# Moving the sampling of a convolution kernel from an expert stage to the stage after it, on one core

## The chip, the cores and the metric

One core of one Trainium2 chip runs the whole program. The metric is the device time of one execution in microseconds; the kernel before took 3562.75 us (median of three runs, 3560.17 to 3565.22). TensorE does the matrix products, ACT (ScalarE), DVE (VectorE) and POOL (GpSimd) work elementwise, and SP issues most of the transfers.

## The reference, cut to what matters

The reference is a decoder of two layers on 4 x 512 tokens of width 256. In each layer an attention, a cross attention and a mixture of experts follow each other, each with a residual and a layer norm behind it. Two of the pieces matter here. The first is layer 0's mixture, in which each token goes to 2 of 8 experts:

```python
g = jax.nn.softmax(h @ Wr, axis=-1)
top2_w, top2_idx = jax.lax.top_k(g, 2)
top2_w = top2_w / jnp.sum(top2_w, axis=-1, keepdims=True)
hid = jax.nn.relu(jnp.einsum('bsh,ehf->bsef', h, W1))
expert_out = jnp.einsum('bsef,efh->bseh', hid, W2)
```

The second is the long convolution of layer 1. Its kernel K depends on weights alone, so it can be made long before it is needed:

```python
dtA = dt[:, None] * A
dC = C * (jnp.exp(dtA) - 1.0) / A
powers = jnp.exp(dtA[:, :, None] * jnp.arange(L))
K = 2.0 * jnp.einsum('dn,dnl->dl', dC, powers).real
Kf = jnp.fft.rfft(K, n=n, axis=-1)
```

d is one of 256 channels, n one of 64 states, l one of 512 positions. A value K[d, l] is called a tap here.

## The kernel before, in words

`l0_ffn` runs layer 0's mixture in four stages: routing, sorting the tokens by expert, the experts (`l0_experts`), and combining with the norm (`l0_combine_and_norm`). Each stage is a block: all engines start it together, and each runs its own list of instructions in order, with waits on semaphores between them.

**The taps.** For every channel the position is split as l = low + 32 x high. For each state (real and imaginary parts on 128 partitions) V holds the powers of the 32 low parts and U those of the 16 high parts, with the coefficients. The taps of one channel are then one product of a 128x32 and a 128x16 matrix. DVE and ACT make V and U in the expert stage, 32 channels at a time: eight chunks (CHUNKS = 8, CW = 32 channels), each in four pieces (`piece`, `growth`, `waves` of `ConvolutionKernel`). One float32 product is two matmul instructions in the trace, so a chunk is 64 of them. V is a tile of its own; U lies in G.branch, which nobody else uses until the stage after the combine.

**The expert stage** (`l0_experts`) runs over 39 slots of 128 sorted rows (SLOTS). For each slot j TensorE does the hidden layer of slot j+1 (L1453, 32 instructions), the transposes of the rows of slot j+2 (L1442) and the output of slot j (L1464, 16 instructions). ACT applies the relu (L1501) and copies rows and results (L1494, L1507); DVE brings the expert's first weights (L1532) and makes a piece of V or U; SP loads rows and the second weights (1 MB a slot) and stores the results. In the second of every four slots from slot 5 on, TensorE also does `taps(c)` for the chunk finished before (L1473), into the PSUM tile pk. Two slots later DVE copies it out with four strided copies (L1543), each a quarter of the high parts into 32 partitions of K.taps. So there are eight slots with taps and 31 without.

**The combine stage** (`l0_combine_and_norm`). POOL issues 32 gathers (L2846), two experts' results for each of 16 token tiles. For each of four batches DVE waits for the batch's eight gathers, adds the weighted results (L2916), takes mean and variance, waits for ACT's square root (`root(b)`, L2888, with one table load), and scales x (L2929). TensorE then transposes the batch (`turn(b)`, L2867) and ACT copies the transposes out (`copies(b)`, L2894). Besides, the taps are taken to the spectrum: eight transforms (L2856), each of eight 128x256 matmul instructions with the DFT matrix, which SP loads when the stage starts; ACT keeps each result (L2883), and SP stores all of it once the eighth is there (L2936). The order is written by hand. On TensorE: transforms 0 to 3, turn(0), transforms 4 to 7, turn(1), turn(2), turn(3). On ACT: keep 0 to 3, root(0), copies(0), keep 4 to 7, root(1), copies(1), and so on.

`made` in `l0_experts` counts the steps of the coefficients, from which the taps' wait for DVE is worked out.

Of the kernel before, what the change touches and what calls it, by code (L numbers as in the profile page):

```python
# [15 lines left out]
B, S, D = 4, 512, 256  # L16
# [25 lines left out]
def buffers(nc, ctx, tag):  # L42

    def sb(name, shape, dt=F32):
        return ctx.enter_context(nc.sbuf_tensor(f"{tag}_{name}", shape, dt))

    def ps(name, shape):
        return ctx.enter_context(nc.psum_tensor(f"{tag}_{name}", shape, F32))

    def sem(name):  # L50
        return ctx.enter_context(nc.semaphore(f"{tag}_{name}"))

    return sb, ps, sem
# [908 lines left out]
LO, HI = 32, 16  # L962
MAGIC = 1.5 * 2 ** 23
TWO_PI = 6.283185
CHUNKS = 8
CW = D // CHUNKS
# [409 lines left out]
def l0_experts(nc, G, R, K):  # L1376

    with ExitStack() as ctx:
        sb, ps, sem = buffers(nc, ctx, "f0")
# [10 lines left out]
        px = ps("px", [P, KD, P])  # L1390
        ph = [ps(f"ph{i}", [P, 512]) for i in range(2)]
        py = [ps(f"py{i}", [P, D]) for i in range(2)]
        pk = ps("pk", [LO, CW, HI])
        tapped, taps_read = sem("tapped"), sem("taps_read")
        made = K.steps[0]
        xs_loaded = [sem(f"xs_loaded{i}") for i in range(3)]
        w2_loaded = [sem(f"w2_loaded{i}") for i in range(2)]
        y_stored = [sem(f"y_stored{i}") for i in range(3)]
# [3 lines left out]
        with nc.Block() as block:  # L1402
# [32 lines left out]
            @block.tensor  # L1435
            def _(pe):
                def turn_rows(j):
                    pe.wait_ge(xs_loaded[j % 3], 16 * (j // 3 + 1))
                    if j >= 1:
                        pe.wait_ge(x_ready, j)  # L1440
                    for k in range(KD):
                        ins = pe.transpose(px[:, k, :], xs[:, j % 3, k * P:(k + 1) * P], G.ident[:])  # L1442
                    ins.then_inc(x_turned, 1)

                def hidden(j):
                    pe.wait_ge(x_ready, j + 1)
                    for half in range(2):
                        if j >= 1:
                            pe.wait_ge(h_done, 2 * (j - 1) + half + 1)
                        pe.wait_ge(w1_brought, 2 * j + half + 1)  # L1450
                        for f in range(HF):
                            for k in range(KD):
                                ins = pe.matmul(ph[half][:, f * P:(f + 1) * P], first[half][:, k, f * P:(f + 1) * P], xsT[:, j % 2, k, :],  # L1453
                                                start=(k == 0), stop=(k == KD - 1))
                        ins.then_inc(h_full, 1)

                def out(j):
                    pe.wait_ge(w2_loaded[j % 2], 16 * (j // 2 + 1))
                    if j >= 2:
                        pe.wait_ge(y_done, j - 1)  # L1460
                    for f in range(FT):
                        if f % HF == 0:
                            pe.wait_ge(h_done, 2 * j + f // HF + 1)
                        ins = pe.matmul(py[j % 2][:], hT[j % 2][:, f * P:(f + 1) * P], w2[:, j % 2, f, :],  # L1464
                                        start=(f == 0), stop=(f == FT - 1))
                    ins.then_inc(y_full, 1)

                def taps(c):
                    pe.wait_ge(K.dve_steps, made + K.STEPS * (c + 1))
                    if c >= 1:  # L1470
                        pe.wait_ge(taps_read, c)
                    for i in range(CW):
                        ins = pe.matmul(pk[:, i, :], K.V[:, CW * c + i, :], K.U[:, CW * c + i, :], start=True, stop=True)  # L1473
                    ins.then_inc(tapped, 1)

                turn_rows(0)
                turn_rows(1)
                hidden(0)
                for j in range(SLOTS):
                    if j + 1 < SLOTS:  # L1480
                        hidden(j + 1)
                    if j + 2 < SLOTS:
                        turn_rows(j + 2)
                    out(j)
                    if j % K.PIECES == 1 and 1 <= j // K.PIECES <= CHUNKS:
                        taps(j // K.PIECES - 1)

            @block.scalar
            def _(act):
# [34 lines left out]
            @block.vector  # L1524
            def _(dve):
                def bring(j):
                    e = dve.value_load(R.expert[0:1, j:j + 1], min_val=0, max_val=E0 - 1)
                    for half in range(2):
                        if j >= 1:
                            dve.wait_ge(h_full, 2 * (j - 1) + half + 1)  # L1530
                        w = R.w1[:, bass.ds(e, 1), :, half * 512:half * 512 + 512].rearrange("p a k f -> p (a k) f")
                        dve.tensor_copy(first[half], w).then_inc(w1_brought, 1)  # L1532

                dve.wait_ge(R.w1_loaded, 16 * E0)
                bring(0)
                for j in range(SLOTS):
                    if j + 1 < SLOTS:
                        bring(j + 1)
                    c = j // K.PIECES - 1
                    if j % K.PIECES == 3 and 0 <= c < CHUNKS:  # L1540
                        dve.wait_ge(tapped, c + 1)
                        for a in range(4):
                            ins = dve.tensor_copy(K.taps[32 * a:32 * a + 32, :, CW * c:CW * c + CW],  # L1543
                                                  pk[:, :, :].rearrange("l c (j a) -> l a j c", a=4)[:, a])
                        ins.then_inc(taps_read, 1)
                    if 0 <= (j - 1) // K.PIECES < CHUNKS:
                        K.piece(dve, (j - 1) // K.PIECES, (j - 1) % K.PIECES)

# [1274 lines left out]
def l0_combine_and_norm(nc, G, R, K):  # L2823

    with ExitStack() as ctx:
        sb, ps, sem = buffers(nc, ctx, "cn")
# [3 lines left out]
        rstd = sb("rstd", [P, TT])  # L2830
        pf = [ps(f"pf{i}", [P, 512]) for i in range(2)]
        pT = [ps(f"pT{i}", [P, NT, P]) for i in range(2)]
        dft_in, spectrum, kept, stored = sem("dft_in"), sem("spectrum"), sem("kept"), sem("stored")
        moments, rooted, x_ready = sem("moments"), sem("rooted"), sem("x_ready")
        turned, copied, dve_steps = sem("turned"), sem("copied"), sem("dve_steps")
# [5 lines left out]
        with nc.Block() as block:  # L2841
# [8 lines left out]
            @block.tensor  # L2850
            def _(pe):
                def transform(m):
                    if m >= 2:
                        pe.wait_ge(kept, m - 1)
                    for k in range(NT):
                        ins = pe.matmul(pf[m % 2][:, 0:D], dft[:, k, m * P:(m + 1) * P], K.taps[:, k, :],  # L2856
                                        start=(k == 0), stop=(k == NT - 1))
                    ins.then_inc(spectrum, 1)

                def turn(b):  # L2860
                    pe.wait_ge(x_ready, NT * (b + 1))
                    for k in range(KD):
                        n = b * KD + k
                        if n >= 2:
                            pe.wait_ge(copied, n - 1)
                        for q in range(NT):
                            ins = pe.transpose(pT[n % 2][:, q, :], G.x[:, b * NT + q, k * P:(k + 1) * P], G.ident[:])  # L2867
                        ins.then_inc(turned, 1)

                pe.wait_ge(dft_in, 16)  # L2870
                for m in range(FT):
                    transform(m)
                turn(0)
                for m in range(FT, 2 * FT):
                    transform(m)
                for b in range(1, B):
                    turn(b)

            @block.scalar
            def _(act):  # L2880
                def keep(m):
                    act.wait_ge(spectrum, m + 1)
                    act.copy(kf[:, m, :], pf[m % 2][:, 0:D]).then_inc(kept, 1)  # L2883

                def root(b):
                    r = slice(b * NT, (b + 1) * NT)
                    act.wait_ge(moments, b + 1)
                    act.activation(std[:, r], rstd[:, r], ACT.Sqrt).then_inc(rooted, 1)  # L2888

                def copies(b):  # L2890
                    for k in range(KD):
                        n = b * KD + k
                        act.wait_ge(turned, n + 1)
                        act.copy(G.xT[:, k, b * S:(b + 1) * S], pT[n % 2][:].rearrange("p a b -> p (a b)")  # L2894
                                 ).then_inc(copied, 1)

                for m in range(FT):
                    keep(m)
                root(0)
                copies(0)  # L2900
                for m in range(FT, 2 * FT):
                    keep(m)
                for b in range(1, B):
                    root(b)
                    copies(b)

# [592 lines left out]
```

## Time and profile before

| | |
|---|---|
| median of three runs | 3562.75 us |
| the profiled execution | 3564.6 us |
| its span, first to last instruction | 3562.8 us |
| mean granted TensorE clock | 0.823 of full |
| TensorE busy | 2771.1 us (78%) |
| DVE busy | 2386.4 us (67%) |
| ACT busy | 1118.4 us (31%) |
| POOL busy | 997.6 us (28%) |

The profile is of one execution. Its times are microseconds from the first instruction. A share of busy time is a mean over stages with different limits; here the two stages of the change lie at 671 to 976 (experts) and 979 to 1032 (combine). PEclk is the granted clock of TensorE as a share of full speed: 1.00 is 2.4 GHz, 0.50 is 1.2 GHz. In a timeline, neighbouring instructions of a kind are merged into one row; the ends of matmuls are modelled, so the spacing of starts is the better measure.

### The profile page before, as it was taken

Reading aid. Unit: us, or ns where it says so; the run is one execution under the profiler, and the core shown is the slowest. Engines: PE = TensorE matmul, PEld = TensorE weight load, DVE = VectorE, ACT = ScalarE, POOL = GpSimd, SP = SyncE. Lnnn points to the kernel's source line nnn. Section 1 sums busy time; section 2 is a strip of 40 time slices with the busy share of each in tenths; the row PEclk is TensorE's granted clock in tenths of the full one; section 3 lists DMA queues with packets and bytes.
Section 4 is the critical chain, followed back from the end, with each engine's and each line's share of the span. In section 5 each row is a group of like instructions: output and inputs, shape, how many; then the busy total and the mean of one; then the engine's idle time right before and its main releaser. Section 6 shows DMA issues by size and latency. Waiting matters only on the chain. (4 is left out here: it accounts for less than half of the span.)

```text
span 3562.8 us, 43681 instructions
## 1 busy us (share of the span) xinstructions
PE 2771.1 (78%) x12600; PEld 1905.2 (53%) x12600; DVE 2386.4 (67%) x8897; ACT 1118.4 (31%) x2893; POOL 997.6 (28%) x1242
## 2 busy tenths in 40 slices
PE   4665995499957667767787668765479999999999
PEld 2223564499834345535464445454436656666666
DVE  4996565466334999899989998999767635212112
ACT  1113562244313333433343334332232123222221
POOL 2552000300032454545454545455312210000000
PEclk7556996699976788787867886867679999999999
DMA  2000002455532211212122211111020032212212
GB/s 96 0 0 14 6 1 104 129 170 164 162 131 92 76 59 63 65 65 69 54 72 68 69 55 67 60 54 35 1 93 1 1 89 67 79 53 63 77 51 68
DMA packets 180780, 235.56 MB, mean 66 GB/s; under 512 B 35761, under 2 KB 138869, under 8 KB 180286
## 3 DMA queue, kind: packets, MB, share of 16 engines
q1 hardware_dynamic: 177470, 224.37, 19.7%
q0 software_dynamic: 3072, 8.39, 0.7%
q8 instruction: 103, 1.69, 0.2%
q14 instruction: 135, 1.11, 0.1%
HBM read 170.57 MB, written 62.13 MB: 65 GB/s over the span
## 5 line engine op out<-in xcount | busy, mean ns | idle before, releaser
L1883 PE MATMUL a_pat<-a_kp,a_probs 128*128 128x128 f32 x1344 | 292.8, 392 | 237.7 <-POOL a_kp L2102 232.7
L1883 PEld LDWEIGHTS a_pat<-a_kp,a_probs 128*128 128x128 f32 x1344 | 259.6, 288 | 317.3 <-POOL a_kp L2102 300.0
L2141 POOL TENSOR_SCALAR a_probs<-a_mixed,a_best 128x120 f32<-128x120 f32 (+12 forms) x208 | 302.4, 1454 | 251.8 <-DVE a_best L2208 115.8
L3408 DVE TENSOR_TENSOR tl_hT<-tl_act_out,tl_gate 128x512 f32<-128x512 f32 x128 | 88.6, 692 | 385.8 <-ACT tl_act_out L3279 385.8
L1864 PE MATMUL a_psc<-a_kT,branch 64*128 64x264 f32 (+3 forms) x640 | 225.6, 603 | 119.5 <-ACT a_stage L1966 118.8
L2194 DVE MAX8 a_best<-a_rest 128x8 f32<-128x208 f32 (+23 forms) x768 | 271.2, 374 | 0.0
L2248 DVE MATCH_REPLACE8 a_rest<-a_best,a_rest 128x104 f32<-128x104 f32 (+31 forms) x732 | 266.0, 373 | 0.0
L2102 POOL TENSOR_SCALAR a_kp<-a_kpost,a_rden 128x128 f32<-128x128 f32 x256 | 152.9, 609 | 386.2 <-DVE a_rden L2215 385.8
L1874 PE MATMUL a_pmix<-a_rows,a_kpre 128*128 128x264 f32 (+41 forms) x528 | 185.8, 482 | 84.2 <-ACT a_mixed L1999 79.7
L2186 DVE MATCH_REPLACE8 a_rest<-a_best,a_rest 128x204 f32<-128x204 f32 (+23 forms) x672 | 245.9, 371 | 0.0
L2256 DVE MAX8 a_best<-a_rest 128x8 f32<-128x104 f32 (+31 forms) x732 | 244.6, 377 | 0.0
L3193 PE MATMUL tl_py<-tl_w,tl_hT 128*128 128x256 f32 x1024 | 241.6, 379 | 0.0
L3174 PE MATMUL tl_ph<-xT,tl_w 128*128 128x512 f32 x512 | 240.7, 592 | 0.0
L3193 PEld LDWEIGHTS tl_py<-tl_w,tl_hT 128*128 128x128 f32 x1024 | 194.6, 190 | 80.2 <-issue 60.0
L1864 PEld LDWEIGHTS a_psc<-a_kT,branch 64*128 64x128 f32 x640 | 118.0, 257 | 212.2 <-ACT a_stage L1966 185.9
L2018 ACT ACTIVATE a_probs<-a_probs,a_negmax 128x72 f32<-128x72 f32 (+28 forms) x232 | 126.1, 545 | 262.4 <-POOL a_probs L2149 259.8
L3279 ACT ACTIVATE tl_act_out<-tl_ph,tl_b 128x512 f32<-128x512 f32 x128 | 88.0, 688 | 351.8 <-PE tl_ph L3174 351.8
L2149 POOL TENSOR_TENSOR a_probs<-a_mixed,a_probs 128x72 f32<-128x72 f32 (+28 forms) x232 | 185.3, 820 | 9.3
L1874 PEld LDWEIGHTS a_pmix<-a_rows,a_kpre 128*128 128x128 f32 x528 | 100.3, 226 | 126.1 <-issue 116.1
L1966 ACT COPY a_stage<-a_psc 128x264 f32<-128x264 f32 (+3 forms) x320 | 112.7, 381 | 121.9 <-PE a_psc L1864 115.7
L1453 PE MATMUL f_ph<-f_xsT,xT 128*128 128x128 f32 x1248 | 148.6, 278 | 0.0
L1453 PEld LDWEIGHTS f_ph<-f_xsT,xT 128*128 128x128 f32 x1248 | 147.0, 195 | 1.7
(465 smaller groups left out, 5643.1 us busy)
## 6 DMA issues: line engine op xcount, KB each, us to landing
f_w<-in_L_ffn_W SPq DMA_DIRECT2D x39, 1024.0 KB, 5.7
tl_gate<-l_gates SPq DMA_DIRECT2D x256, 128.0 KB, 2.9
l_scores<-a_stage SPq DMA_DIRECT2D x32, 528.0 KB, 2.7
l_scores<-a_stage SPq DMA_DIRECT2D x32, 400.0 KB, 2.4
l_scores<-a_stage SPq DMA_DIRECT2D x32, 272.0 KB, 2.1
f0o_w<-in_L_ffn_W SPq DMA_DIRECT2D x8, 1024.0 KB, 12.9
sorted_x<-z_blank SPq DMA_DIRECT2D x1, 4992.0 KB, 15.6
f_xs<-sorted_x SPq DMA_DIRECT2D x39, 128.0 KB, 5.3
```

The costliest lines, as they stand in the source:

```text
L1453: ins = pe.matmul(ph[half][:, f * P:(f + 1) * P], first[half][:, k, f * P:(f + 1) * P], xsT[:, j % 2, k, :], start=(k == 0), stop=(k == KD ...
L1864: full(pe.matmul(out[:, 0:hi - lo], qT[r, j, i * P:(i + 1) * P], kT[r, j, lo:hi], start=True, stop=True))
L1874: ins = pe.matmul(pmix[:, at, 0:hi - lo], kpre[:], rows[:, g % 4, lo:hi], start=True, stop=True)
L1883: ins = pe.matmul(pat[:, at + c, :], probs[:, g % 4, c * P:(c + 1) * P], kp[:, g % 4, :], start=True, stop=True)
L2141: ins = pool.tensor_scalar(p, x, best[:, a, LAST, 7:8], HIDE, ALU.is_lt, ALU.mult)
L2149: pool.tensor_tensor(p, x, p, ALU.add).then_inc(masked, 1)
L2186: last[a, part] = signal(dve.match_replace(values, top, values, GONE))
L2194: ins = dve.max(best[:, a, q, :] if part == 0 else low[:, a, 8 * q + 1:8 * q + 9], values)
L2248: last[a] = signal(dve.match_replace(rest[:, a, 0:wd], best[:, a, q - 1, :], rows_of[a] if q == 1 else rest[:, a, 0:wd], GONE))
L2256: last[a] = signal(dve.max(best[:, a, q, :], rest[:, a, 0:wd]))
L3174: ins = pe.matmul(ph[m % 2][:], lhsT, G.xT[:, k, b * S:(b + 1) * S], start=(k == 0), stop=(k == KD - 1))
L3193: ins = pe.matmul(py[t][:, 0:D], src[:, t * P:(t + 1) * P], w, start=(n == 0), stop=False)
```

## The change

The taps' matmuls leave the expert stage, and DVE's copies of them with them. In the combine stage TensorE does all eight chunks first, into two PSUM tiles in turn; ACT copies each chunk out with four copies. turn(0) now follows the taps, then transforms 0 to 3, turn(1), transforms 4 to 7, turn(2) and turn(3); ACT's order is changed to match: copies of the taps, root(0), copies(0), keep 0 to 3, root(1), copies(1), keep 4 to 7, root(2), and so on. The transforms wait until all the taps are copied. TensorE no longer waits for DVE's steps before the taps, since the stage change covers that.

```diff
@@ l0_experts
-        pk = ps("pk", [LO, CW, HI])
-        tapped, taps_read = sem("tapped"), sem("taps_read")
-        made = K.steps[0]
...
-                def taps(c):
-                    pe.wait_ge(K.dve_steps, made + K.STEPS * (c + 1))
-                    if c >= 1:
-                        pe.wait_ge(taps_read, c)
-                    for i in range(CW):
-                        ins = pe.matmul(pk[:, i, :], K.V[:, CW * c + i, :], K.U[:, CW * c + i, :], start=True, stop=True)
-                    ins.then_inc(tapped, 1)
-
...
-                    if j % K.PIECES == 1 and 1 <= j // K.PIECES <= CHUNKS:
-                        taps(j // K.PIECES - 1)
...
-                    c = j // K.PIECES - 1
-                    if j % K.PIECES == 3 and 0 <= c < CHUNKS:
-                        dve.wait_ge(tapped, c + 1)
-                        for a in range(4):
-                            ins = dve.tensor_copy(K.taps[32 * a:32 * a + 32, :, CW * c:CW * c + CW],
-                                                  pk[:, :, :].rearrange("l c (j a) -> l a j c", a=4)[:, a])
-                        ins.then_inc(taps_read, 1)
@@ l0_combine_and_norm
+        pk = [ps(f"pk{i}", [LO, CW, HI]) for i in range(2)]
+        tapped, taps_read = sem("tapped"), sem("taps_read")
...
+                for c in range(CHUNKS):
+                    if c >= 2:
+                        pe.wait_ge(taps_read, c - 1)
+                    for i in range(CW):
+                        ins = pe.matmul(pk[c % 2][:, i, :], K.V[:, CW * c + i, :], K.U[:, CW * c + i, :], start=True, stop=True)
+                    ins.then_inc(tapped, 1)
+                turn(0)
                 pe.wait_ge(dft_in, 16)
+                pe.wait_ge(taps_read, CHUNKS)
                 for m in range(FT):
                     transform(m)
-                turn(0)
+                turn(1)
                 for m in range(FT, 2 * FT):
                     transform(m)
-                for b in range(1, B):
+                for b in range(2, B):
                     turn(b)
...
+                for c in range(CHUNKS):
+                    act.wait_ge(tapped, c + 1)
+                    for a in range(4):
+                        ins = act.copy(K.taps[32 * a:32 * a + 32, :, CW * c:CW * c + CW],
+                                       pk[c % 2][:, :, :].rearrange("l c (j a) -> l a j c", a=4)[:, a])
+                    ins.then_inc(taps_read, 1)
+                root(0)
+                copies(0)
                 for m in range(FT):
                     keep(m)
-                root(0)
-                copies(0)
+                root(1)
+                copies(1)
                 for m in range(FT, 2 * FT):
                     keep(m)
-                for b in range(1, B):
+                for b in range(2, B):
                     root(b)
                     copies(b)
```

## Rows read from the trace of the kernel before

**Rows 1.** Who waited for whom, expert stage, 672 to 979: total, times, longest.
```profile
ACT xT L1501 <- PE f_ph L1453: 119.7, 78, 3.8
DVE xT L1532 <- PE f_ph L1453: 93.5, 46, 7.1
...
PEld f_pk L1473 <- DVE sk_angle L1112: 2.3, 7, 0.3
```

**Rows 2.** Timeline of TensorE, one slot with taps and one without: start, us, what.
```profile
718.80 3.62 PE L1464 MATMUL f_py<-f_w,xT 128*128 128x256 f32 x16
722.35 2.20 PE L1473 MATMUL f_pk<-branch,sk_V 128*32 128x16 f32 x64
724.48 3.84 PE L1453 MATMUL f_ph<-f_xsT,xT 128*128 128x128 f32 x32
...
728.37 3.62 PE L1464 MATMUL f_py<-f_w,xT 128*128 128x256 f32 x16
...
735.62 3.62 PE L1464 MATMUL f_py<-f_w,xT 128*128 128x256 f32 x16
```

**Rows 3.** Timeline of all engines, combine stage: start, us, what [idle before <-releaser].
```profile
987.67 9.18 PE L2856 MATMUL cn_pf<-f0o_taps,f0o_w 128*128 128x256 f32 x32 [11.57 <-DMA f0o_w<-in_c_dft]
...
991.98 3.38 DVE L2916 SCALAR_TENSOR_TENSOR x<-f0o_w,f0o_gates,x 128x256 f32<-128x256 f32 x8 [29.20 <-DMA f0o_w<-sorted_y,f0o_slot]
...
997.28 1.28 ACT L2888 ACT_TABLE_LOAD   x1
...
998.57 0.21 ACT L2888 ACTIVATE cn_std<-cn_rstd 128x4 f32<-128x4 f32 x1
...
1000.68 1.09 PE L2867 MATMUL cn_pT<-ident,x 128*128 128x128 f32 x8 [3.82 <-DVE x L2929]
...
1001.61 8.76 PE L2856 MATMUL cn_pf<-f0o_taps,f0o_w 128*128 128x256 f32 x32
...
1010.40 0.37 ACT L2883 COPY f0o_w<-cn_pf 128x256 f32<-128x256 f32 x1 [1.35 <-PE cn_pf L2856]
1010.67 0.21 ACT L2888 ACTIVATE cn_std<-cn_rstd 128x4 f32<-128x4 f32 x1
...
1012.56 1.09 PE L2867 MATMUL cn_pT<-ident,x 128*128 128x128 f32 x8 [2.20 <-DVE x L2929]
...
1017.89 0.20 ACT L2888 ACTIVATE cn_std<-cn_rstd 128x4 f32<-128x4 f32 x1 [3.56 <-DVE cn_rstd L2925]
...
1021.89 3.38 DVE L2916 SCALAR_TENSOR_TENSOR x<-f0o_w,f0o_gates,x 128x256 f32<-128x256 f32 x8 [2.09 <-DMA f0o_w<-sorted_y,f0o_slot]
...
1027.37 0.20 ACT L2888 ACTIVATE cn_std<-cn_rstd 128x4 f32<-128x4 f32 x1 [4.91 <-DVE cn_rstd L2925]
...
1031.26 0.59 ACT L2894 COPY xT<-cn_pT 128x512 f32<-128x512 f32 x1 [0.27 <-PE cn_pT L2867]
```

**Rows 4.** Groups of instructions by line, expert stage: busy us, mean ns | idle before.
```profile
L1543 DVE COPY f0o_taps<-f_pk 32x128 f32<-32x128 f32 x32 | 8.9, 279 | 0.3
```

**Rows 5.** Stretches: us, PE, PEld, DVE, ACT, POOL busy (count), PEclk, DMA share, GB/s.
```profile
976.00:978.00 2.00, 0.10 (x1) 0.00 (x0) 0.00 (x0) 0.37 (x1) 0.00 (x0) 1.00 0.19 66
978.00:980.00 2.00, 0.00 (x0) 0.00 (x0) 0.00 (x0) 0.00 (x0) 0.60 (x1) 0.53 0.23 29
1002.00:1004.00 2.00, 2.00 (x6) 1.58 (x6) 1.96 (x6) 0.44 (x1) 1.39 (x3) 0.50 0.23 74
1004.00:1006.00 2.00, 2.00 (x7) 1.59 (x7) 1.97 (x6) 0.37 (x1) 1.70 (x2) 0.64 0.44 129
600.00:605.00 5.00, 5.00 (x25) 5.00 (x25) 0.00 (x0) 0.98 (x1) 0.00 (x0) 0.50 1.03 410
```

**Rows 6.** Timeline of TensorE, the last of the router's logits: start, us, what.
```profile
598.85 6.83 PE L1224 MATMUL r_pl<-r_wr,xT 128*128 128x8 f32 x32
```

**Rows 7.** Groups of ACT by line and shape: busy us, mean ns | idle before.
```profile
L2029 ACT COPY a_aT_small<-a_pat 128x128 f32<-128x128 f32 x64 | 16.7, 268 | 42.4 <-PE a_pat L1883 42.1
```

**Rows 8.** Transfers by line, 960 to 1060: KB each, median us to landing.
```profile
s4d_spectrum<-f0o_w SPq DMA_DIRECT2D x1, 1024.0 KB, 4.7
```

## The prediction

> **What bounds the kernel now.** I read the waits of the expert stage first. ACT and DVE both wait for TensorE there, and in tens of microseconds; what TensorE waits for on their account is next to nothing [rows 1]. The timeline of TensorE says the same: the matmuls of one slot start where those of the slot before end, and a slot takes 728.37 to 735.62, so 7.25 us [rows 2]. In such a stage every instruction taken off TensorE shortens the stage by its own spacing.
>
> The combine stage is another kind. DVE's first combine waits 29.20 us for the first of POOL's 32 gathers. TensorE waits 11.57 us for the DFT matrix and has the first four transforms out of the way before DVE has normalised anything. Only one place is held up by TensorE: root(1) comes at 1010.67, right behind the copy of the eighth transform at 1010.40. Batch 3 starts at 1021.89, after 2.09 us of waiting for its gathers, so the tail is set by the gathers, which land 11 us after the last transform is out. The last copy ends at 1031.85 [rows 3]. TensorE has idle time in this stage, but in pieces, and ACT is in the chain: DVE asks it for a square root once in every batch.
>
> **What is removed.** A slot with taps goes from 718.80 to 728.37, 9.57 us, against 7.25 without: 2.32 us for a chunk, of which 2.13 lie between the chunk's first matmul and the next slot's [rows 2]. Eight chunks give 8 x 2.32 = 18.6 us. DVE's 32 copies of 279 ns go too [rows 4]; DVE waits for TensorE already [rows 1], so they are worth nothing by themselves. Would another engine take over the stage at 7.25 us for all 39 slots? Three of every four slots already run at that pace with the same loads and the same pieces of the kernel's making, so I take the whole 18.6. The next to be late would be DVE's copy of the weights; it is idle before most of these copies. Bounds: 18.6 at most, 0 if a queue that only recovers in the tap slots were the limit.
>
> **What is added on TensorE.** The same 8 x 64 matmuls now come first in the combine stage. Times from here on are counted from 978.7, the stage's start. What they cost depends on the clock. TensorE is busy for 0.10 us of the 2 from 976, still at 1.00, and in the 2 us from 978 the clock is at 0.53, nearly all at 1.2 GHz [rows 5]; it will be idle as long in the new kernel, since the stage change is the same. So the taps start at 1.2 GHz, or fall to it within a chunk. Do they win the 2.4 GHz back? The DFT transforms do: started at 1001.61, they run at 0.50 from 1002 to 1004 and at 0.64 over the next 2 us, so the clock rises in that stretch [rows 3, 5]. But those stream 256 columns behind each load of weights. The router's logits stream 8: they keep TensorE busy for 5.00 of the 5 us from 600 and it stays at 0.50 throughout [rows 5]. The taps stream 16 columns behind 32 columns of weights. In make they are nearer to the logits, and I take the whole stream at 1.2 GHz.
>
> The Trainium skill, "TensorE: Matmul & The Clock Gate", section "Part 1: The HAM clock gate", says that throttling is the default and that sustained matmul activity releases it. Read plainly, a back-to-back stream of taps would release it, which is my first rival; the logits' row disagrees.
>
> The price of a tap at 1.2 GHz: no row has it. From below it is the price at full clock, 2.13 us for 64; from above twice that, 4.26. The nearest row is again the logits': 32 in 6.83 us, 213 ns each, the time of loading 128 columns of weights, with their few moving columns hidden [rows 6]. A tap loads 32 columns, a quarter: 53.3 ns, 3.41 us a chunk. Eight take 27.3 us; I take off 0.3 for the part of the first chunk that may still find the full clock: the taps end at 27.0.
>
> **What is added on ACT.** Four copies for a chunk. ACT's copy of 128x128 from PSUM takes 268 ns [rows 7]; a tap copy has 128 elements a partition too, but strided; DVE pays 279 for the same pattern [rows 4]. 4 x 0.27 = 1.1 us, under the 3.4 of a chunk and with two PSUM tiles, so only the last chunk's copies show: 27.0 + 0.2 + 1.1 = 28.3. If striding costs ACT double, it is 1.1 more; up to 3.4 us a chunk it stays hidden but for the last. Behind the wait for the taps ACT has root(0), and DVE waits for that. The table load of 1.28 us, which stood right ahead of the root at 997.28 [rows 3], now follows the copies: root(0) at 29.6. Before, it was at 998.57, which is 19.9.
>
> **How the order moves the rest.** Step by step, with the spacings of [rows 3].
> - root(0) to turn(0) takes 998.57 to 1000.68, 2.1 us: turn(0) at 31.7 (before 22.0). By then the gathers of batch 1 have long landed.
> - turn(0), four transforms, then root(1). The transforms took 8.76 us from 1001.61, about 3.8 of them at half clock (all up to 1004, and 1.4 of the 2 us at a mean of 0.64) [rows 5], so about 6.9 at full clock; the turn is 0.9 more. Again with 3.8 us at half clock: 7.8 + 1.9 = 9.7. root(1) follows 0.3 behind: 41.7 (before 32.0). DVE's moments for batch 1 need 5.5 us after its start (1021.89 to 1027.37 for batch 3), so they are ready at 37.2 and wait for ACT, as they did.
> - root(1) to turn(1) 1.9 us: 43.6. The other four transforms now stand here, ahead of root(2) on ACT; before, root(2) came at 1017.89 with no transform in its way. 7.8 us if the clock is kept over the 2 us of idleness (it was, at 1012.56: 1.09 us for eight transposes), 9.7 if not; I take 8.3, and 0.3 for the copy: root(2) at 52.2. The moments of batch 2 were ready at 43.6 + 5.5 = 49.1, so this is a new stall of 3.1 us. The first four transforms no longer hide under the gathers: that is what is late next.
> - root(2) to the start of batch 3: 1.8 us (DVE is free 0.1 before the turn starts), 54.0. Its gathers landed at 43.2, so the 2.09 us wait goes. Moments 5.5: root(3) at 59.5. From there to the stage's end 1027.37 to 1031.85, 4.5: 64.0.
> Before, the end was at 1031.85 - 978.7 = 53.15. The stage grows by 10.8 us.
>
> The DFT matrix's load is not moved, and its wait of 11.57 us disappears under the taps. POOL's gathers stay as they are. SP's store of the spectrum is issued behind the eighth transform, at 52 instead of 32; it lands 4.7 us later [rows 8], 57, seven before the stage ends, and nothing but the barrier is behind it. If it took over 12 us it would show.
>
> **The sum.** -18.6 + 10.8 = -7.8 us. The profiled execution took 3564.6 us for a span of 3562.8, 1.8 for what lies around it, so the new one would be 3556.8; the median of the runs shown is 3562.75, 1.85 below the profiled execution, and from there I get **3554.9**. If the clock rises sooner or later under the transforms, each of the two groups takes 7.8 to 9.7 us, and the taps' first chunk may save up to 1.3: 3551.5 to 3558. With 4.26 us for a chunk the taps end 6.8 later: 3561.7. What this kernel's measurement can tell from no change is about 0.2%, 7.1 us, so 3555.6 is the line and the forecast lies just beyond it.
>
> **Rivals.**
> (a) *The taps win the full clock back.* For: in the expert stage they run at full clock, 64 in 2.13 us [rows 2]. Against: the logits [rows 5]. Taps end at 17.1, copies and table load by 19.7, root(0) not later than before's 19.9, and the first four transforms fall exactly where the last four lay. What is left is the order: root(2) behind the last four transforms, at 32.0 + 1.9 + 7.8 + 0.3 = 42.0 with the clock kept, 43.9 without, against 39.2; batch 3 starts at 43.8 to 45.7 against 43.2. The stage grows by 0.6 to 2.5: about 3545.7, a gain of 17.
> (b) *A chunk costs 4.26 us at the low clock*, because whatever makes the 33 ns at full clock scales whole: 3561.7, within 0.2%.
> (c) *The copies take over* (the other side). ACT reads PSUM with a stride, in 32 partitions. If four copies take longer than a chunk's 3.41 us, ACT sets the pace: it starts at 3.6 and is through at 3.6 + 8 x the four. The gain is gone when that is 7.8 later than 28.3, at 4.06 us for four (1.0 a copy), and the kernel is slower by over 7.1 us from 4.95 (1.24 a copy) on. With five times DVE's 279 ns, 1.4 a copy, the copies end at 48.4, 20.1 late: 3575. DVE's own price for the pattern speaks against it [rows 4].
> (d) *The expert stage does not shrink* by 18.6, since the loads of w2 or DVE's pieces hold it: with half of it, 3564.2, no change. The tap-free slots speak against it.
>
> **Chances.** The forecast, taps at half clock with some 3.4 us a chunk: 0.70. (a) 0.11, (b) 0.10, (c) 0.05, (d) 0.04. The forecast's own range, 3551.5 to 3558, lies across the line of 3555.6; about 0.6 of its chance is below. Faster by over 0.2%: 0.7 x 0.62 + 0.11 + a little = 0.55. Slower: (c), and the worse half of (d): 0.06. Same: 0.39. The range takes in (b), most of (d) and the step towards (a): 3547 to 3564; outside are most of (a) and (c).
>
> **What would show it.** In the changed kernel: 39 slots of 7.25 us with no break; the taps at a granted clock of 0.50 and about 53 ns apart; ACT's copies near 0.27 us; root(0) near 29.6 and root(2) near 52 after the stage's start, with DVE waiting for ACT some 3 us before the latter; no DMA wait before batch 3; a stage of 64 us against 53. I am wrong if the clock rises within the taps, if a tap is nearer 67 ns, if a copy takes over 0.8 us, or if slots are longer than 7.25.

## The result, and the profile after

The changed kernel takes 3553.3 us (median of nine runs, 3549.9 to 3558.6), the kernel before 3560.2 in the same comparison (nine runs, 3554.1 to 3565.5): a ratio of 0.9977, with a 95% interval of 0.9969 to 0.9986, which is 5 to 11 us. It is faster by 6.9 us where 7.8 were forecast.

The profiled execution has a span of 3556.7 us against 3562.8. TensorE's timeline of the expert stage in the changed kernel (start, us, what; lines of the kernel after the change) shows three slots and the end:

```profile
930.25 3.62 PE L1461 MATMUL f_py<-f_w,xT 128*128 128x256 f32 x16
...
937.50 3.62 PE L1461 MATMUL f_py<-f_w,xT 128*128 128x256 f32 x16
...
944.74 3.62 PE L1461 MATMUL f_py<-f_w,xT 128*128 128x256 f32 x16
...
951.77 7.07 PE L1461 MATMUL f_py<-f_w,xT 128*128 128x256 f32 x32
```

All slots now follow each other after 7.25 us, as the tap-free ones did before [rows 2]. From the first slot's output matmul to the last slot's it was 289.9 us and is 271.3: 18.6 us off, as forecast.

The timeline of all engines in the combine stage, which answers to [rows 3]:

```profile
961.48 0.39 SPq L2932 DMA_DIRECT2D f0o_w<-in_c_dft  x1
961.52 27.29 PE L2856 MATMUL cn_pk<-branch,sk_V 128*32 128x16 f32 x512 [2.68 <-PEq L1399]
...
973.74 3.38 DVE L2914 SCALAR_TENSOR_TENSOR x<-f0o_w,f0o_gates,x 128x256 f32<-128x256 f32 x8 [28.22 <-DMA f0o_w<-sorted_y,f0o_slot]
...
988.85 1.05 ACT L2890 COPY f0o_taps<-cn_pk 32x128 f32<-32x128 f32 x4 [2.37 <-PE cn_pk L2856]
989.92 1.28 ACT L2878 ACT_TABLE_LOAD   x1
991.21 0.20 ACT L2878 ACTIVATE cn_std<-cn_rstd 128x4 f32<-128x4 f32 x1
991.45 0.18 DVE L2925 RECIPROCAL cn_rstd<-cn_std 128x4 f32<-128x4 f32 x1 [12.27 <-ACT cn_std L2878]
...
993.25 1.97 PE L2849 MATMUL cn_pT<-ident,x 128*128 128x128 f32 x8 [4.44 <-DVE x L2927]
...
995.01 9.20 PE L2838 MATMUL cn_pf<-f0o_taps,f0o_w 128*128 128x256 f32 x32
...
1004.52 0.21 ACT L2878 ACTIVATE cn_std<-cn_rstd 128x4 f32<-128x4 f32 x1
...
1007.35 7.07 PE L2838 MATMUL cn_pf<-f0o_taps,f0o_w 128*128 128x256 f32 x32
...
1014.72 0.21 ACT L2878 ACTIVATE cn_std<-cn_rstd 128x4 f32<-128x4 f32 x1
...
1014.97 0.18 DVE L2925 RECIPROCAL cn_rstd<-cn_std 128x4 f32<-128x4 f32 x1 [3.26 <-ACT cn_std L2878]
...
1016.47 3.38 DVE L2914 SCALAR_TENSOR_TENSOR x<-f0o_w,f0o_gates,x 128x256 f32<-128x256 f32 x8
...
1021.95 0.20 ACT L2878 ACTIVATE cn_std<-cn_rstd 128x4 f32<-128x4 f32 x1 [3.56 <-DVE cn_rstd L2923]
...
1025.84 0.58 ACT L2884 COPY xT<-cn_pT 128x512 f32<-128x512 f32 x1 [0.27 <-PE cn_pT L2849]
```

The reader should see four things. The 512 tap matmuls take 27.29 us, 53.3 ns each. ACT's four copies take 1.05 us and from the second chunk on wait 2.37 for TensorE each time. DVE waits 12.27 us for ACT's first root, with its first batch's moments ready. And root(2), at 1014.72, stands right behind the last transform's copy, with DVE waiting 3.26 us for it; batch 3 has no DMA wait left. The stretches answer to [rows 5]:

```profile
961.00:966.00 5.00, 4.48 (x88) 4.51 (x89) 0.00 (x0) 1.01 (x4) 2.92 (x4) 0.58 0.69 229
966.00:971.00 5.00, 5.00 (x98) 5.00 (x96) 0.00 (x0) 1.02 (x5) 3.78 (x5) 0.50 0.92 348
976.00:981.00 5.00, 5.00 (x98) 5.00 (x97) 3.08 (x12) 1.26 (x5) 3.84 (x4) 0.50 0.38 110
```

TensorE is busy without a gap and its clock stays at 0.50, 1.2 GHz. The stage now takes 64.9 us (961.48 to 1026.42) against 53.1 (978.71 to 1031.85).

So the difference of the two spans, -6.1 us, is made of: expert stage from its first matmul to the next stage's start 307.50 to 288.36, -19.1 (18.6 from the slots, 0.5 ahead of the first slot's output, where the clock rose sooner after the first matmul); combine stage +11.8; +1.9 ahead of the experts and -0.7 behind the stage, in parts that the change does not touch.

### The profile page after: what moved, and what is told of

It reads as the page before. It is cut to its first block and busy times, and to the rows that moved or that the text cites. A ratio compares the mean times of both kernels' runs of the same rounds, so it can differ in the third digit from the quotient of the medians.

```text
span 3556.7 us, 43675 instructions
## 1 busy us (share of the span) xinstructions
PE 2778.7 (78%) x12600; PEld 1918.1 (54%) x12600; DVE 2377.6 (67%) x8865; ACT 1126.4 (32%) x2925; POOL 995.6 (28%) x1242
```

## The experiments

In the table are times from the start of the combine stage (SP's load of the DFT matrix) to the start of each root on ACT and to the end of the last copy, from each run's timeline. Kernels are named as in the headings below. The last eight rows are from other chips, on which something else happens (see E6 and E7).

| kernel | root(0) | root(1) | root(2) | root(3) | stage |
|---|---|---|---|---|---|
| before | 19.9 | 32.0 | 39.2 | 48.7 | 53.1 |
| changed | 29.7 | 43.0 | 53.2 | 60.5 | 64.9 |
| E1, no taps | 20.5 | 33.5 | 40.7 | 48.4 | 52.9 |
| E2, wide | 21.1 | 33.7 | 44.0 | 51.2 | 55.7 |
| E3, roots first | 29.7 | 37.4 | 44.8 | 52.0 | 55.7 |
| E4, both | 18.3 | 28.4 | 38.2 | 49.6 | 54.1 |
| E5, second chip | 62.1 | 74.8 | 85.0 | 92.2 | 96.7 |
| E6, second chip | 59.2 | 66.4 | 73.8 | 85.9 | 89.6 |
| before, third chip (E7) | 23.5 | 51.6 | 58.9 | 66.1 | 70.6 |
| changed, third chip (E8) | 68.9 | 81.4 | 91.7 | 98.9 | 103.4 |
| E6 again, third chip (E9) | 58.6 | 65.8 | 73.3 | 85.4 | 89.1 |
| E4 again, third chip (E10) | 59.5 | 69.7 | 76.9 | 84.1 | 88.6 |
| E11, fourth chip | 45.2 | 76.9 | 88.8 | 96.0 | 100.5 |
| E12, fourth chip | 58.7 | 66.0 | 73.2 | 85.1 | 88.8 |

### E1: the kernel before without taps

```diff
-                    if j % K.PIECES == 1 and 1 <= j // K.PIECES <= CHUNKS:
-                        taps(j // K.PIECES - 1)
...
-                        dve.wait_ge(tapped, c + 1)
-                        for a in range(4): ...
+                dve.memset(K.taps[:], 0.0)
```

> The kernel before with the taps left out altogether (K.taps is zero, so the convolution has no kernel): it measures what the removal alone is worth. My theory: TensorE sets the pace of the expert stage, each slot is 7.25 us, and the whole is 8 x 2.32 = 18.6 us shorter than the kernel before, with a combine stage of 53.1 us as before. Rival: part of the gain is lost in the slots or behind them, and less than 15 us come off.

Measured: 3543.7 us against 3556.6, ratio 0.9961 (0.9948 to 0.9975). That is 13.0 us, and the interval, 9 to 18.5 us, just misses the 18.6; by the medians the rival (less than 15) would hold. The total scatters by some microseconds from parts that no edit touches (see the end). The trace is sharper: from the first slot's output matmul to the last slot's it is 271.3 us against 289.9, from TensorE's first instruction in the stage to the last slot's output 285.6 against 304.5, and the combine stage is 52.9, as before. Within the two stages the removal is worth its full price.

### E2: wider moving operand

```diff
-                        ins = pe.matmul(pk[c % 2][:, i, :], ..., K.U[:, CW * c + i, :], ...)
+                        two = min(i + 2, CW)
+                        ins = pe.matmul(pk[c % 2][:, i:two, :], ..., K.U[:, CW * c + i:CW * c + two, :], ...)
```

> The changed kernel, with every tap matmul streaming 32 columns of U in place of 16 (each one also writes the next channel's place, which the next one overwrites), the same 32 columns of weights. My theory: at 1.2 GHz the price of a tap is that of its weights, so the wider stream costs nothing there; and it is the thin stream that leaves the clock at 1.2 GHz, so now the clock rises within the first two chunks, the later taps are some 32 ns apart, all taps take 18 to 19.5 us in place of 27.3, root(0) comes 8 to 9 us earlier, and the stage is 55 to 57 us in place of 65: 8 to 10 us faster than the changed kernel, about 16 below the kernel before. Rival one: the clock stays low because of the weight loads or the stage change, whatever is streamed: same time as the changed kernel, 53 ns a tap. Rival two: the columns are paid for in full: 80 to 107 ns a tap at the low clock, 14 us or more slower.

Measured: 3543.5 us, ratio 0.9961 (0.9948 to 0.9975). The stretches of E2:

```profile
958.00:960.00 2.00, 2.00 (x42) 2.00 (x41) 0.00 (x0) 0.33 (x2) 1.39 (x3) 0.50 0.94 348
960.00:962.00 2.00, 2.00 (x63) 2.00 (x61) 0.00 (x0) 0.69 (x3) 1.52 (x2) 0.90 0.99 395
962.00:964.00 2.00, 2.00 (x69) 2.00 (x67) 0.00 (x0) 1.02 (x4) 1.56 (x2) 1.00 1.04 412
```

42 taps reach into two microseconds at 0.50, as many as of the thin ones, then 69 at 1.00. The taps' matmuls do twice the multiplications, and root(0) comes 8.7 us earlier and the stage is 9.2 shorter than in the changed kernel; by the medians it is 13.1 below the kernel before, where the changed kernel was 6.9 below. Both rivals fall: with the same weight loads and the same stage change the clock rises once 32 columns are streamed in place of 16, and the added columns cost nothing at either clock.

### E3: only ACT's order

```diff
                 copies(0)
-                for m in range(FT):
+                keep(0)
+                root(1)
+                for m in range(1, FT):
                     keep(m)
-                root(1)
                 copies(1)
+                root(2)
                 for m in range(FT, 2 * FT):
                     keep(m)
-                for b in range(2, B):
-                    root(b)
-                    copies(b)
+                root(3)
+                copies(2)
+                copies(3)
```

> The changed kernel with ACT's order alone changed: the square roots stand ahead of the copies of transforms (root(1) behind the first, root(2) ahead of the last four, root(3) ahead of the last transposes). My theory: of the 11.8 us by which the combine stage grew, the taps' lateness makes 9.7 at root(0), but 6 of these would be absorbed by the wait for the last gathers, and ACT's order makes the rest. So root(0) stays at 29.6, root(1) comes at 37, root(2) at 44.7, and the stage is 56.6 us: 8 us faster than the changed kernel. Rival: the lateness of the taps is what counts and the order only 2 us; the gain over the changed kernel is then 2 us or less.

Measured: 3543.2 us, ratio 0.9958 (0.9944 to 0.9972). ACT's timeline:

```profile
991.55 0.20 ACT L2878 ACTIVATE cn_std<-cn_rstd 128x4 f32<-128x4 f32 x1
...
999.02 0.37 ACT L2873 COPY f0o_w<-cn_pf 128x256 f32<-128x256 f32 x1 [2.83 <-PE cn_pf L2838]
999.29 0.21 ACT L2878 ACTIVATE cn_std<-cn_rstd 128x4 f32<-128x4 f32 x1
...
1006.67 0.20 ACT L2878 ACTIVATE cn_std<-cn_rstd 128x4 f32<-128x4 f32 x1 [0.54 <-DVE cn_rstd L2925]
```

The taps are as slow and root(0) as late as in the changed kernel, 29.7, yet the stage is 55.7 us: of the 11.8 us, 9.2 went with the order of three small activations. Where the 9.8 us by which root(0) is late go can be read from the table, row of E3 against the kernel before: 5.4 are left at root(1), which no longer stands behind four transforms, 5.6 at root(2), 3.3 at root(3), since batch 3 no longer waits for its gathers, and 2.6 at the end. The wait for the last gathers absorbs some 2 us of the lateness, then, and not 6, as was expected; most went at root(1). E2 took away the same 9.2 from the other side, so the two gains don't add: either one leaves 2.6, and both together (E4) leave 1.0.

### E4: both, and root(0) ahead of the last chunk's copies

```diff
                 for c in range(CHUNKS):
+                    if c == CHUNKS - 1:
+                        root(0)
                     act.wait_ge(tapped, c + 1)
```

> Both together, with root(0) also ahead of the last chunk's copies. My theory: no root waits for TensorE's work, the last gathers set the end again (batch 3 waits for its DMA), the stage is 53 to 54 us as in the kernel before, and all 18.6 us of the expert stage are kept: 3541.6 us against 3560.2, as fast as the kernel without taps. Rival: the taps still delay something, and it stays 3 us or more above the kernel without taps.

The other roots stand on ACT as early as their moments can be there: root(1) ahead of the copy of transform 3, root(2) ahead of that of transform 6, root(3) behind the last transposes' copies of batch 2.

Measured: 3537.8 us, ratio 0.9939 (0.9924 to 0.9953): 18.8 us below the kernel before, the fastest of all on that chip. DVE's last batch waits for its gathers again:

```profile
999.83 3.38 DVE L2921 SCALAR_TENSOR_TENSOR x<-f0o_w,f0o_gates,x 128x256 f32<-128x256 f32 x8 [4.15 <-DMA f0o_w<-sorted_y,f0o_slot]
```

The stage is 54.1 us, 1.0 over the kernel before, since the wait for the last gathers ends 1.0 later (44.1 against 43.2), though POOL starts the last of them as early as before (40.1 against 40.3); whether the spectrum's store, now beside them, did that was not tried.

### E5: wide for three chunks, thin for five

```diff
-                        two = min(i + 2, CW)
+                        two = min(i + 2, CW) if c < 3 else i + 1
```

> The changed kernel with 32 streamed columns for the first three chunks and 16 for the other five. The clock rises within the first two chunks, as the run with all eight wide showed. The question is whether the thin stream can hold the full clock once it has it. Theory one, it cannot: within a few us of the fourth chunk the spacing goes back from 32 to 53 ns, the taps end at about 23 to 25 us, the stage is 60 to 63 us. Theory two, it holds: the taps end at 18 to 19.5 and the stage is 56 us, as with all eight wide.

### E6: thin taps, orders laid so that no root waits

```diff
                     ins.then_inc(tapped, 1)
+                    if c == CHUNKS - 2:
+                        turn(0)
-                turn(0)
+                turn(1)
...
                 for c in range(CHUNKS):
+                    if c == CHUNKS - 3:
+                        root(0)
+                    if c == CHUNKS - 1:
+                        copies(0)
+                        root(1)
                     act.wait_ge(tapped, c + 1)
```

All eight transforms stand behind turn(1); ACT goes on with copies(1), keep(0), root(2), keep(1) to keep(7), root(3), copies(2), copies(3).

> The changed kernel's thin taps, with the orders laid so that no root waits: on TensorE seven chunks, the transposes of batch 0, the eighth chunk, the transposes of batch 1, all eight transforms, the rest; on ACT root(0) ahead of the copies of chunk 5, root(1) ahead of those of chunk 7, root(2) behind the first transform's copy, root(3) behind the last. My theory: the clock as such cost nothing that an order can't hide: the taps still run at 53 ns and end near 29 us, but root(0) comes at 19.9, root(1) at 28.5, root(2) at 35 to 37, batch 3 waits for its gathers, and the stage is 53 to 55 us: 11 faster than the changed kernel and 18 below the kernel before. Rival: the slow taps push transforms and transposes past the gathers' end, and the stage is 57 us or more.

Measured: E5 3590.4 us, E6 3582.3, and the kernel before 3580.6: ratios 1.0031 (1.0019 to 1.0043) and 1.0007 (0.9998 to 1.0016). Neither expectation says anything of this. The group ran on another chip than E1 to E4, and there the kernel before is itself 24 us slower. TensorE's timeline of E6:

```profile
962.14 3.92 PE L2856 MATMUL cn_pk<-branch,sk_V 128*32 128x16 f32 x78 [2.67 <-PEq L1399]
966.37 0.25 PE L2856 MATMUL cn_pk<-branch,sk_V 128*32 128x16 f32 x2 [0.31 <-issue]
...
985.60 0.19 PE L2856 MATMUL cn_pk<-branch,sk_V 128*32 128x16 f32 x1 [2.59 <-issue]
...
1007.30 0.19 PE L2856 MATMUL cn_pk<-branch,sk_V 128*32 128x16 f32 x1 [0.52 <-issue]
1008.00 17.68 PE L2856 MATMUL cn_pk<-branch,sk_V 128*32 128x16 f32 x329 [0.51 <-issue]
```

After 78 taps TensorE waits for nothing but its own issue, in steps of 0.7 us or multiples of it, until 1008; then 329 run without a gap, 54 ns apart. POOL's last gather is issued at 1001.92. The stage is 90 us, and the 53 to 55 that were expected could not be tried.

E5's question of the clock was answered all the same, once its stall was over, at 1005.68. 396 matmuls of the taps were left then, 76 of them wide and, from the fourth chunk on, 320 thin. Its stretches from 1008 on:

```profile
1008.00:1010.00 2.00, 2.00 (x62) 2.00 (x60) 0.00 (x0) 0.60 (x3) 0.00 (x0) 0.89 0.00 0
1010.00:1012.00 2.00, 2.00 (x69) 2.00 (x66) 0.00 (x0) 0.99 (x5) 0.00 (x0) 1.00 0.00 0
1016.00:1018.00 2.00, 2.00 (x69) 2.00 (x67) 0.00 (x0) 1.00 (x4) 0.00 (x0) 1.00 0.04 8
```

The last 320 matmuls are 32 ns apart: the thin stream holds the full clock for 10 us once it has it, though it had not won it in 27. In E6, on the same chip, the 329 thin ones behind the stall stayed at 0.50 for their 17.68 us. Theory two was right on the clock; its times, 56 us for the stage, are those of a chip without the stall.

### E7 to E10: is it the chip or the kernel?

> The kernel before, profiled again beside the others of this group. In the last group everything ran on another chip: the kernel before took 3580.6 us there against 3556.6, and in both experiments TensorE's taps stalled between 965 and 1008 us, in steps of 0.7 us, for as long as POOL's gathers ran. If that belongs to the chip and not to the two kernels, then on such a chip this kernel too has stretches in which TensorE waits for its own issue, of 20 us in all; on a chip like the first it has none and takes 3555 to 3562.

> The changed kernel again. If the stall belongs to the chip: on a chip like the first 7 us below the kernel before, combine stage 65 us, no stall; on a chip like the second its taps stall beside the gathers too, the stage is 95 to 100 us, and the kernel is 10 to 15 us slower than before. If the stall belonged to the two kernels of the last group: a stage of 65 us on either.

> Thin taps with the orders laid so that no root waits, again. If the stall belongs to the chip, then on one like the first: root(0) at 19.9, stage 53 to 55 us, 18 below the kernel before, as was expected of it the first time; on one like the second 90 us again. If it belongs to this kernel: 90 us on either.

> Wide taps with the roots first, again. On a chip like the first 54 us and 18 to 19 below the kernel before; on one like the second, if the stall belongs to the chip, its taps stall beside the gathers too and its gain of 18 turns into no change or a loss.

All four ran on a third chip, and it has the stall too. Medians against the kernel before, 3581.6 us there: before again 3581.2 (ratio 1.0001), **changed 3593.2, ratio 1.0043 (1.0026 to 1.0060)**, E6 again 3579.2 (0.9998, 0.9988 to 1.0008), E4 again 3577.9 (0.9996, 0.9986 to 1.0006). So the stall does not belong to the two kernels of the last group: the kernel before has it too, without any taps there. I call it the chip's; but each of these chips was used in one group of runs only, so a chip and its hour can't be told apart. Which chip the comparison of the result ran on is not on record; neither of its two profiles has the stall. The waits of the kernel before in its combine stage there:

```profile
DVE cn_rstd L2927 <- ACT cn_std L2888: 21.5, 3, 21.0
...
ACT f0o_w L2883 <- issue: 14.6, 1, 14.6
ACT f0o_w L2883 <- remote: 14.6, 2, 9.3
...
DVE cn_rstd L2927 <- issue: 5.6, 1, 5.6
```

and those of the changed kernel:

```profile
ACT f0o_taps L2890 <- PE cn_pk L2856: 41.9, 3, 37.2
PEld cn_pk L2856 <- issue: 40.2, 31, 3.1
PE cn_pk L2856 <- issue: 35.8, 24, 2.6
```

```profile
q0 software_dynamic: 1488, 4.07, 36.8%
q1 hardware_dynamic: 253, 0.97, 6.5%
q8 instruction: 4, 0.07, 0.7%
q14 instruction: 1, 0.01, 0.1%
```

and on the third chip, 963 to 1003, where no packet of an instruction queue is listed at all:

```profile
q0 software_dynamic: 1536, 4.20, 34.9%
q1 hardware_dynamic: 242, 0.93, 5.7%
```

It is the same in the other traces: none during the stall of the taps in E5, E6, E9, E10 and E12, but four on q8 beside the gathers in E2, E3 and E4, as in the first list. In E7 one packet is listed between 990 and 993, and ACT, held up since 978, goes on at 992.84. So the engines seem to wait for their instructions to be loaded. That the gathers hold this load back, and why on some chips alone, isn't shown: in E8 and E11 the next packet is listed only after the engine has gone on.

### E11: gathers behind the taps

```diff
             def _(pool):
+                pool.wait_ge(taps_read, CHUNKS)
                 for t in range(TT):
```

> The changed kernel with POOL's gathers held back until all taps are copied out, so that nothing is gathered beside the taps. Theory: the stall of the taps comes from the gathers running beside them. Then the taps take 27.3 us with no gap on any chip, and the gathers' own 40 us come behind: a stage of about 28.5 + 53 = 81 to 84 us on a chip like the first (before: 53), and there 9 to 12 us slower than the kernel before; on a chip like the second and third some stalls of ACT and DVE return once the gathers run, as in the kernel before, 90 to 100 us. Rival: the thin stream itself, or the load of the DFT matrix beside it, starves TensorE's issue on such chips; the gaps of 0.7 us and more are in the taps again.

A fourth chip, with the stall: 3592.2 us, ratio 1.0035 (1.0024 to 1.0047). TensorE's timeline and, below it, ACT's:

```profile
960.38 26.81 PE L2857 MATMUL cn_pk<-branch,sk_V 128*32 128x16 f32 x512 [2.69 <-PEq L1399]
```

```profile
988.30 1.28 ACT L2879 ACT_TABLE_LOAD   x1
1005.52 0.21 ACT L2879 ACTIVATE cn_std<-cn_rstd 128x4 f32<-128x4 f32 x1 [15.94 <-issue]
```

With no gathers beside them the 512 taps take 26.8 us without a gap, though the DFT matrix is being loaded, and four instruction packets are listed meanwhile. The rival is out: in E12, on the same chip, the taps beside the gathers have their gaps again. The gathers start at 988.55, and at once it is ACT's turn to wait 15.94 us for its issue; later it is TensorE's, ahead of a transform:

```profile
1022.32 3.78 PE L2839 MATMUL cn_pf<-f0o_taps,f0o_w 128*128 128x256 f32 x8 [7.87 <-issue]
```

The stage is 100.5 us, at the upper end of what was expected. The stall comes with the gathers, whatever is put beside them. Its mechanism stays open; so does whether the recording of the profile takes part in it.

### E12: thin taps between, a third time

> Thin taps with the orders laid so that no root waits, a third time, since the first two fell on chips with the stall. On a chip like the first: taps at 53 ns without a gap, root(0) at 19.9, root(1) at 28.5, a stage of 53 to 55 us, 18 below the kernel before. On a chip with the stall: 90 us again, level with the kernel before.

The same chip as E11: 3581.8 us, ratio 1.0001 (0.9991 to 1.0011), a stage of 89 us, as on the two others, with gaps of up to 2.62 us in the taps. What E6 gives on a chip without the stall was not measured.

## Why the prediction was right, and what it missed

Step by step, the forecast in brackets where two numbers stand together.

- *What is removed*, 18.6 us: measured 18.6, and E1's slots confirm it; rival (d) is out.
- *The clock*: the taps ran at 1.2 GHz for 27 us on end, as forecast from the logits [rows 5]; rival (a), which would have given 17 us of gain, is out, and in E2, with 32 columns streamed and nothing else changed, the clock rose. The Trainium skill's rule ("TensorE: Matmul & The Clock Gate", section "Part 1: The HAM clock gate") is that sustained activity releases the clock. Read as back-to-back instructions, this trace doesn't agree with it: 27.29 us without a gap at 0.50.
- *The price of a tap*: 53.3 ns forecast as a quarter of the logits' 213 [rows 6], 27.29 us for 512 measured; the 0.3 us I took off for the first chunk was not there. Rival (b) is out.
- *ACT's copies*: 1.05 us for four, 1.1 forecast; rival (c) is out.
- *The order*: root(0) at 29.7 (29.6), root(1) at 43.0 (41.7), root(2) at 53.2 (52.2), root(3) at 60.5 (59.5), stage 64.9 (64.0).

The mis-sized term is the first group of transforms: with its transposes it took from 993.25 to the root at 1004.52, 11.3 us in place of 10.0. I had priced the transposes at full clock, 0.9 us, and only the transforms at half clock to begin with. But the clock that the taps had left at 0.50 was still there: the transposes took 1.76 us to the first transform (993.25 to 995.01), 0.8 more, and 4.2 us of the transforms ran at half clock in place of 3.8, which is 0.4. The stretches show when it rose:

```profile
997.00:999.00 2.00, 2.00 (x6) 1.55 (x6) 1.54 (x8) 0.33 (x1) 1.39 (x3) 0.50 0.37 109
999.00:1001.00 2.00, 2.00 (x10) 1.73 (x9) 0.00 (x0) 0.24 (x2) 1.70 (x2) 0.92 0.43 117
```

The second group stayed at full clock, 8.3 us from transposes to root in place of 8.6. The new stall of DVE behind root(2) is 3.26 us; forecast 3.1. The vanished DMA wait before batch 3 and the hidden store were right too: the stage ends in transposes and copies, not in a wait for the store.

So the sum was -18.6 + 10.8 and is -18.6 + 11.8; the medians give -6.9. The stages in the trace bear the sum out step by step; the medians alone, with an interval of 5 to 11 us, could not. The upper end of the forecast's own range, 3558, doesn't follow from its terms, which add 1.4 us for the second group and 0.3 for the first chunk: 3556.6. And the line of 0.2% that was named is met at 0.23%, with an interval of 0.14 to 0.31%: that the time lies beyond the line is partly luck.

What the prediction had no place for is that the number doesn't hold on every chip. On the third the same change is 0.43% slower, by a mechanism that none of my rivals names: engines that wait for their issue while the gathers run. The sum's step "POOL's gathers stay as they are" was true of the gathers and silent on what happens to a thousand instructions put beside them. No row of the kernel before, profiled on a chip without the stall, shows it.

I had also seen only one of two levers. Rival (a) says what the stage grows by if the taps run at full clock, 0.6 to 2.5 us, and E2 measured 2.6. What ACT's order gives by itself I never asked, though the sum holds both of its steps, root(1) and root(2) behind the transforms' copies; E3 shows that moving three roots on ACT, at no cost, gives back 9.2 of 11.8 us, with the taps as slow as ever.

## What to carry to other kernels

Before work is moved into the idle time of an engine, look at the in-order queues around it: here the engine that only copies (ACT) also serves the chain's small square roots, and putting each root ahead of the bulk copies was worth as much (9.2 us, E3) as speeding up the taps themselves (9.2, E2). The taps' matmuls could be widened from 16 to 32 moving columns for nothing, and the wider stream won the full clock back: where a stream of thin matmuls sits at half clock, that is worth a try. And a stage with many instructions beside gathers should be timed on more than one chip.

## What the runs showed of the hardware

- At 1.2 GHz a stream of 16 columns behind 32 columns of weights took 53.3 ns a matmul and never regained 2.4 GHz in 27 us; 32 columns behind the same weights took 53 ns too, and the clock was up some 4 us after the start (0.90 in the stretch from 960, E2). At 2.4 GHz both take 32 ns, and the thin one held that clock for 10 us (E5).
- On three of four chips of the experiments TensorE, ACT and DVE waited for their own issue while POOL's indirect gathers ran: TensorE by up to 2.6 us between two taps and 7.9 ahead of a transform (E11), ACT by up to 15.9 us (E11), DVE by 5.6 (E7), and the kernel before took 3581 us there against 3557. POOL itself keeps its 1.25 us a gather. During the taps' stall no packet of an instruction queue is listed; on the first chip four are. On the first chip such a step was seen once, 0.68 us in the taps of E2.
- Parts that no edit touched differ by some microseconds between executions: the first expert matmul starts between 667.2 and 673.5 us over the profiles of the two kernels and of E1 to E4. A piece of it can be seen in the router's logits, whose first 16 matmuls took 2.1 us in the kernel before and 3.4 in the changed one, at different clocks. It doesn't explain the whole: E4 has the 3.4 too, and the earliest start of all. For a gain of 7 us the length of the stage is a better witness than the total.
